# The expert results of a mixture-of-experts layer: summed in a DRAM array by the scatter, or reloaded and summed on VectorE

## The reference

```python
x = x + xattn(layernorm(x), ctx_1024, ...)      # cross attention to 4 x 4096 keys
x = x + attn(layernorm(x), ...)                 # windowed attention, 16 heads
x = x + ffn(layernorm(x), ...)                  # mixture of experts

# ffn, x_flat = [1024, 256], E = 8 experts, inner width 1024, K = 2 chosen for each token
top_v, top_i = jax.lax.top_k(x_flat @ gate_w.T, K)
probs = jax.nn.softmax(top_v)
combine = einsum('tk,tke->et', probs, one_hot(top_i, E))
for e in range(E):
    hidden = silu(x_flat @ wg[e].T) * (x_flat @ wu[e].T)
    acc += combine[e][:, None] * (hidden @ wd[e].T)
```

## Time and profile before

| what | value |
|---|---|
| time, median of 3 runs | 676.44 us (675.77 to 679.74) |
| the profiled execution: its own time | 675.65 us |
| its span, first to last instruction | 673.9 us |
| TensorE busy | 607.7 us, 90% |
| VectorE busy | 467.7 us, 69% |
| ScalarE busy | 336.0 us, 50% |
| GpSimd busy | 238.8 us, 35% |
| mean granted TensorE clock | 0.966 of full speed |
| moved by DMA | 153.61 MB, 228 GB/s over the span |

### The profile page before, as it was taken

The page is one execution under the profiler, slowest core; times in us unless marked ns, Lnnn a source line. Parts: engine busy times, 40 slices in busy tenths (PEclk is TensorE's granted clock), DMA queues, the critical chain, the costliest instruction groups (busy, mean ns, idle before and its releaser), DMA issues. The chain is left out here.

```text
span 673.9 us, 10790 instructions
## 1 busy us (share of the span) xinstructions
PE 607.7 (90%) x3988; PEld 515.9 (77%) x3988; DVE 467.7 (69%) x815; ACT 336.0 (50%) x597; POOL 238.8 (35%) x315
## 2 busy tenths in 40 slices
PE   7997999899989999998988864899999999999990
PEld 5676998699878988995656653688888888888880
DVE  4387659757876688767876857577677677677644
ACT  3434742463247524554666660465565565565530
POOL 3002862377218732784643423022222221221210
PEclk9999999999999999998999976899999999999996
DMA  8977689768977937571000334689899999999726
GB/s 280 290 273 219 191 257 354 204 175 245 341 209 201 262 95 218 147 198 39 1 1 2 126 125 157 239 312 343 320 356 342 326 352 341 326 353 337 289 79 195
DMA packets 64996, 153.61 MB, mean 228 GB/s; under 512 B 7728, under 2 KB 45168, under 8 KB 54064
## 3 DMA queue, kind: packets, MB, share of 16 engines
q1 hardware_dynamic: 62736, 146.89, 65.5%
q0 software_dynamic: 2208, 6.03, 2.4%
HBM read 122.56 MB, written 30.34 MB: 227 GB/s over the span
## 5 line engine op out<-in xcount | busy, mean ns | idle before, releaser
L615 ACT ACTIVATE wide_high<-region_a 128x1024 fp32r<-128x1024 f32 (+1 forms) x108 | 102.3, 987 | 106.7 <-PE psum L1543 106.7
L1079 DVE TENSOR_TENSOR wide_low<-region_a,wide_high 128x1024 fp32r<-128x1024 f32 x92 | 108.4, 1221 | 21.2 <-ACT wide_high L615 21.2
L544 POOL TENSOR_TENSOR wide_low<-region_a,wide_high 128x512 fp32r<-128x512 f32 x64 | 82.7, 1294 | 17.7 <-ACT wide_high L615 13.7
L1342 PE MATMUL psum<-turned_high,wide_low 128*128 128x256 f32 x256 | 79.6, 311 | 7.6 <-POOL wide_low L544 3.8
L1557 PE MATMUL psum<-region_a,region_w 128*128 128x256 f32 x368 | 83.3, 379 | 0.3 <-ACT region_w L615 0.3
L1543 PE MATMUL psum<-wide_high,turned_low 128*128 128x512 f32 x184 | 78.8, 428 | 3.6 <-DVE wide_low L1079 2.6
L1185 PE MATMUL psum<-ident,region_s 128*128 128x128 f32 x500 | 70.7, 275 | 8.0 <-ACT region_s L662 5.5
L1557 PEld LDWEIGHTS psum<-region_a,region_w 128*128 128x128 f32 x368 | 68.2, 190 | 8.9 <-issue 0.5
L1543 PE MATMUL psum<-wide_high,turned_high 128*128 128x512 f32 x184 | 73.7, 401 | 0.0
L1543 PE MATMUL psum<-wide_low,turned_high 128*128 128x512 f32 x184 | 73.6, 400 | 0.0
L615 ACT ACTIVATE wide_high<-psum 128x512 fp32r<-128x512 f32 x64 | 34.3, 598 | 78.3 <-PE psum L1304 68.6
(11 more groups left out here) (199 smaller groups left out, 1221.0 us busy)
## 6 DMA issues: line engine op xcount, KB each, us to landing
region_a<-turned_up SPq DMA_DIRECT2D x23, 2048.0 KB, 8.5
region_a<-turned_down SPq DMA_DIRECT2D x23, 1024.0 KB
region_a<-ctx_dram SPq DMA_DIRECT2D x16, 1024.0 KB, 10.2
turned_up<-region_w SPq DMA_DIRECT2D x64, 256.0 KB, 4.1
region_w<-L_ffn_wg_dram SPq DMA_DIRECT2D x16, 512.0 KB, 6.0
region_w<-L_ffn_wu_dram SPq DMA_DIRECT2D x16, 512.0 KB, 6.0
region_w<-L_ffn_wd_dram SPq DMA_DIRECT2D x16, 512.0 KB, 5.9
turned_down<-region_w SPq DMA_DIRECT2D x32, 256.0 KB, 4.2
```

The lines of the kernel that those rows point to most:

```text
L544: nc.gpsimd.tensor_tensor(val_lo[:, g % 4], ctx_sb[n][:, g * PAIR:(g + 1) * PAIR, :], val_hi[:, g % 4].bitcast(F32), ALU.subtract).then_in ...
L615: return nc.scalar.activation(dst, src, ACT.Copy)
L1079: nc.vector.tensor_tensor(w_lo[:, g % 3], whole, w_hi[:, g % 3].bitcast(F32), ALU.subtract).then_inc(low_ready, 1)
L1342: last = nc.tensor.matmul(bank[6 + c][:, 0:NTOK], v[:, g % 4, k, c * P:(c + 1) * P], p[:, g % 2, k, :], start=g == 0 and k == 0 and m == 0 ...
```

## The change

`results_by_token` is gone. In its place stands `sums_by_token` (`sum_dram`, 1024 rows and 128 spare ones). SyncE fills its first 1024 rows from `xr` with one transfer of 1 MB, issued between `load_up(1)` and `load_up(2)`, behind a wait for `heads_added`. The scatter goes by `tokens` instead of `targets` and carries `compute_op=ALU.add`: the transfer itself adds each row to what the DRAM row holds. The first scatter waits for the fill (`sums_begun`). Two tiles that hold results of the same token never run at once, since each scatter waits for the one before, as it did. When the last has landed, one transfer copies the first 1024 rows to the output, DRAM to DRAM. The 8 loads, the 16 additions and the 8 stores are gone, and so is `targets`: the constants of the place computation now give the token at once, in two VectorE instructions. `normed_rows` has 128 spare rows instead of 64.

```diff
-SPARE = P // 2
+SPARE = P
-RESULTS = TOK * TOPK
...
-        y_dram = nc.dram_tensor("results_by_token", [RESULTS + P, D], F32).ap()
+        sum_dram = nc.dram_tensor("sums_by_token", [TOK + SPARE, D], F32).ap()
...
             load_up(1)
+            sp.wait_ge(heads_added, len(LAST_ROWS))
+            sp.dma_start(sum_dram[0:TOK, :].rearrange("(t p) d -> p t d", p=P), xr).then_inc(sums_begun, 16)
             for j in range(2, SLOT_TILES):
...
-            for t in range(TILES):
-                sp.dma_start(y_of[:, t].rearrange("p k d -> p (k d)"),
-                             y_dram[t * P * TOPK:(t + 1) * P * TOPK, :].rearrange("(p k) d -> p (k d)", k=TOPK)).then_inc(y_loaded[t], 16)
-            for t in range(TILES):
-                sp.wait_ge(out_ready, t + 1)
-                sp.dma_start(out.rearrange("b (t p) d -> p (b t) d", p=P)[:, t, :], x3n[:, t, :]).then_inc(out_stored, 16)
-            sp.wait_ge(out_stored, 16 * TILES)
+            sp.dma_start(out.rearrange("b (q r) d -> (b q) (r d)", q=P // BATCH),
+                         sum_dram[0:TOK, :].rearrange("(q r) d -> q (r d)", q=P)).then_inc(out_stored, 16)
+            sp.wait_ge(out_stored, 16)
...
                 pool.wait_ge(y_ready, j + 1)
+                if j == 0:
+                    pool.wait_ge(sums_begun, 16)
...
                 pool.indirect_dma_start(
-                    out=y_dram, out_offset=bass.IndirectOffsetOnAxis(ap=target[:, j:j + 1], axis=0),
-                    in_=yt[n], in_offset=None).then_inc(y_stored[n], 16)
+                    out=sum_dram, out_offset=bass.IndirectOffsetOnAxis(ap=token[:, j:j + 1], axis=0),
+                    in_=yt[n], in_offset=None, compute_op=ALU.add).then_inc(y_stored[n], 16)
...
-            then(nc.vector.tensor_tensor(target[:, :], beside[:, :], found[:, 1], ALU.add))
-            nc.vector.tensor_scalar(token[:, :], target[:, :], 1, None, ALU.logical_shift_right).then_inc(tokens_ready, 1)
+            nc.vector.tensor_tensor(token[:, :], beside[:, :], found[:, 1], ALU.add).then_inc(tokens_ready, 1)
...
-            for t in range(TILES):
-                dve.wait_ge(y_loaded[t], 16)
-                then(nc.vector.tensor_tensor(x3n[:, t, :], y_of[:, t, 0, :], y_of[:, t, 1, :], ALU.add))
-                nc.vector.tensor_tensor(x3n[:, t, :], x3n[:, t, :], xr[:, t, :], ALU.add).then_inc(out_ready, 1)
```

More of the change, by code:

```diff
@@ L134, in perceiver @@
         hidT, yt, silu = [hidT0, hidT1], [yt0, yt1], [silu0, silu1]
-        y_f = region_a[:, 0:2 * TILES * D]
-        y_of = y_f.rearrange("p (t k d) -> p t k d", k=TOPK, t=TILES)
         xr_t = sb("residual", TILES * D)
@@ L214, in perceiver @@
         weight = sb("weights", SLOT_TILES)
-        target, token = sb("targets", SLOT_TILES, I32), sb("tokens", SLOT_TILES, I32)
+        token = sb("tokens", SLOT_TILES, I32)
         steps = sb("steps", E)
@@ L275, in perceiver @@
         y_stored = [sem(f"y_stored{n}") for n in range(2)]
-        y_loaded = [sem(f"y_loaded{n}") for n in range(TILES)]
+        sums_begun = sem("sums_begun")
         paused = sem("paused")
-        out_ready, out_stored = sem("out_ready"), sem("out_stored")
+        out_stored = sem("out_stored")
         rooms = [pv_done, scores_done, probs_turned, *w_stored, probsT_ready, scores_out, x1_ready]
@@ L435, in _ @@
             nc.gpsimd.memset(zeros, 0.0).then_inc(consts, 1)
-            nc.gpsimd.iota(spare_row[:, :], pattern=[[0, 1]], base=RESULTS, channel_multiplier=1,
+            nc.gpsimd.iota(spare_row[:, :], pattern=[[0, 1]], base=TOK, channel_multiplier=1,
                            allow_small_or_imprecise_dtypes=True).then_inc(consts, 1)
@@ L439, in _ @@
                            allow_small_or_imprecise_dtypes=True).then_inc(consts, 1)
-            nc.gpsimd.iota(way_base[:, :].rearrange("p (n t) -> p n t", n=TOPK), pattern=[[1, TOPK], [0, TILES]], base=0,
-                           channel_multiplier=TOPK, allow_small_or_imprecise_dtypes=True).then_inc(consts, 1)
-            nc.gpsimd.iota(ways[:, :, 1].rearrange("p (n t) -> p n t", n=TOPK), pattern=[[0, TOPK], [P * TOPK, TILES]], base=-RESULTS,
+            nc.gpsimd.iota(way_base[:, :].rearrange("p (n t) -> p n t", n=TOPK), pattern=[[0, TOPK], [0, TILES]], base=0,
+                           channel_multiplier=1, allow_small_or_imprecise_dtypes=True).then_inc(consts, 1)
+            nc.gpsimd.iota(ways[:, :, 1].rearrange("p (n t) -> p n t", n=TOPK), pattern=[[0, TOPK], [P, TILES]], base=-TOK,
                            channel_multiplier=0, allow_small_or_imprecise_dtypes=True).then_inc(consts, 1)
```

## The result

The changed kernel takes 673.76 us (median of 13 runs, 670.39 to 679.19), the kernel before, run beside it, 679.47 us (13 runs, 674.26 to 682.97). The ratio is **0.9949, with a 95% interval from 0.9925 to 0.9974**: 0.5% faster, some 3.5 us (1.8 to 5.1), where the prediction said 0.8% and 5.3 us. The forecast's ratio, 0.9921, lies just outside the interval. The ratio on record is not the quotient of the two medians, which is 0.9916 (5.7 us); 13 runs of each don't fix the size to better than a microsecond or two. I had given most of the chance to "within 1%", which it is, and had taken 1% for what a measurement can tell from no change; the interval reaches only 0.25% to each side and leaves out a ratio of 1.

What follows compares the result with a forecast made beforehand. TensorE sets the loop's pace, DMA close behind; the replaced end is wholly exposed. 12.5 + 0.2 - 6.2 - 1.2 = 5.3 us less, median 676.44 to 671.1 us, range 668.3 to 677.0.

Steps and rivals of the forecast that it cites:

- within 1%: Whole kernel: the time changes by under 1% (6.8 us) either way; chance 0.68.
- The end: After the last scatter: 12.5 us of loads, additions and stores go, one DRAM copy of 6.2 us (4.8 to 8) comes.
- x: Last scatter: extra time for reading and adding its DRAM rows, 1.2 us, bounds 0.2 to 3.7, counted only once.
- The loop: Expert rounds: each adding scatter takes 0.34 us more DMA engine time, covered by idle time and slack; cost 0.
- the 0.95 that I gave as the most: Loop: sign that the DMA share rises from 0.91 to no more than 0.95.
- The slow rival: Loop: adding scatters fill the DMA engines, adding 26 to 53 us (692 to 719), from 0.9 us extra engine time; chance 0.12.
- the rate-based end of my bound: Loop: idle DMA time in a 10.0 us round, 2.3 us by rate, against 0.9 us by share.
- Cost 0, with up to 0.5 us for the range: Loop's begin: the 1.05 MB fill behind the second up load delays nothing; 0 us, at most 0.5.
- if the first gather lands late behind the fill: Loop's begin: a sign that would show the prediction wrong; the first gather was expected to be issued at about 411.5.
- The third up load: Loop's begin: sign that this load is issued at about 423.9, where it was 424.12.
- Rival 1: End: x at 0.25 and the copy at 4.8 us, gain 7.6 us, 668.8 us; chance 0.20.
- Rival 3: End: the copy costs what it replaces, 676.4 us; chance 0.06.

Runs made afterwards that it cites:

- the plain scatter: The changed kernel with a scatter that overwrites instead of adding; ratio to the kernel before 0.9933.
- one more adding scatter: The changed kernel with a second adding scatter, of zeros into its own array, in each of the first 21 rounds; ratio to the kernel before 0.9959.
- the early fill: The changed kernel with the fill of the sums issued ahead of the wait for the owners, not behind the second up load; ratio to the kernel before 0.9938.
- the three kernels with more dummy products and the new scatter: The changed kernel with six TensorE dummy products instead of four, 0.9964; with fill ahead of the owners' wait and five, 0.9919, repeated 0.9929.
- The fill alone: The kernel before plus the 1 MB fill at the changed kernel's place, into an array nobody reads; first scatter waits for it; ratio 1.0048.
- the four adding scatters with the gather ahead: The changed kernel with three extra adding scatters in each of the first 21 rounds, each round's gather issued before them; ratio to the kernel before 1.0245.
- the old scatter (with five dummies): The kernel before with five TensorE dummy products instead of four ahead of the first turn; ratio 1.0011.
- Early fill and five dummy products: The changed kernel with the fill ahead of the owners' wait and five TensorE dummy products instead of four; ratios to the kernel before 0.9919, repeated 0.9929.

## Why the prediction was off

**The end: right, with the copy a little cheaper.** The 12.5 us taken away are 12.5 (12.9 with the closing 0.4). The copy was put at 6.2 us, from 4.8 to 8; it took 5.5, of which 2.0 are fixed by the line above, an estimate.

**The adding scatter: right.** x was put at 1.2 us and is 1.3, half of it in GpSimd's instruction, and it counts once. That the read would overlap the work on other rows, for which x was put near its lower bound, was my estimate; no run shows the overlap by itself. That only the last one would count also held: with the plain scatter the rounds take 214.89 us, with the adding one 214.74.

**The loop: the time right, the sizes wrong.** Cost 0 held. But I sized an adding scatter as a doubled plain one, 0.68 us of engine time, and it is more: 14.5% of 185 us is 26.8 us; less 18 gathers of 0.34 this leaves 1.1 us for each of 19 scatters. The packets go with it. The queue's packets on the page went from 2208 to 4416, and are 2208 again with the plain scatter: 48 for each gather or plain scatter on the mean, 144 for an adding one, as many as its 128 rows and the 16 engines together. So the share rose to 0.98, over the 0.95 that I gave as the most, and the up loads' worst case left 0.8 us (12.6 from issue to first use, 11.8 to landing).

**The slow rival: rightly set aside, but by the wrong threshold.** By the share, an estimate, a row costs an engine 1.1 us / 9 packets = 0.12 us, not 0.5; no row here shows directly how two additions overlap. I said that the rival decides from 0.9 us of extra engine time at the earliest. The change itself added 0.75, and one more adding scatter came to 1.9 with 0.8 us lost in all 21 rounds. With four, 4.0 us over the plain one, the program lost 20 us even with the gathers ahead, but there GpSimd's time had run out too. So 0.9 us was too low; no run shows where the threshold lies above 1.9, and the rate-based end of my bound, 2.3 us, isn't contradicted. The rival's times were also added up wrongly: 26 to 53 us on top of the forecast's 671.1 are 697 to 724, and my 692 to 719 took the gain of 5.3 us off twice.

**The step that failed** is "Cost 0, with up to 0.5 us for the range", for the fill where the loop begins, and its ground, that the gather "shares the engines with `load_up(1)` either way, and the fill is behind that". The fill cost 0.9 us of the stretch in the changed kernel (1.1 with the 0.2 us that the removed instruction gave back) and 0.8 us in the kernel before. I had shown that no load was late behind it and took a place in SyncE's queue for a place in time. The fill's own length was forecast well: it was to end 12.2 us behind the place computation and landed 12.3 us behind it (issued at 415.61, 12.3 us to landing, counted from 415.57). That its traffic and the first gather's would meet had no price. The prediction had named this sign, "if the first gather lands late behind the fill", and it came; so did a DMA share over 0.95. The third up load was to come 0.2 us earlier; counted from the place computation it came 1.8 us later (15.8 us behind it instead of 14.0).

**What stays open.** Put together, the profiles give 12.5 + 0.2 - 5.5 - 1.3 - 1.2 = 4.7, and 4.9 with the small differences in the rounds, against a forecast of 5.3. So the copy gave 0.7 us more than forecast, and the late gather's 1.2 took that and more. The runs give 3.5, from 1.8 to 5.1. The 1.4 us between them are within that interval, but they have a pattern: in the early fill, the plain scatter and the kernel with one more adding scatter, too, the ratio shows 0.8 to 1.5 us less gain than the profile counted from `spare_or_way`, and in the three kernels with more dummy products and the new scatter 2.6 to 2.8 us less. The fill alone and the four adding scatters with the gather ahead go the same way, by 3.0 and 4.0 us. These signs are not independent, since the ratios of one batch share the same runs of the kernel before, and they hang on how the runs are summed up: by the medians the changed kernel gains 0.8 us more than its profile shows, and the early fill, the plain scatter, the one more adding scatter and the three with more dummy products 0.1 to 1.6 us less. The second profile of the old scatter (with five dummies) has 263.94 us from there to the end, like the first with 263.75, so it is not one odd profile of before. The rest would have to lie ahead of that instruction, where the profiles spread over 9 us with the clock and one of each kernel can't show 1 us, or in executions unlike the profiled ones. It stays open.

Rival 1 (a better end) did not come: copy and x together are 6.8 us, over the 5.9 from which the gain passes 1%. Rival 3, with its chance of 0.06, was a copy that costs what it replaces, with a time of 676.4 us. No row or run shows a rate or a fixed cost that would make a copy so long; it took 5.5 us where 12.5 went away.

**The better version.** Early fill and five dummy products make it 0.9919 and 0.9929 to the kernel before. In both measurements the upper end is below 1; against the changed kernel the difference is likely but not settled.

## What to carry to other kernels

A tail of loads, sums and stores can become one DRAM copy behind adding scatters: here 12.5 us became 5.5, for 1.3 us more on the last scatter. Ask what the adding scatters cost in the steady loop twice over, in DMA engine time (here a packet a row) and in GpSimd's own time (1.6 us for each instead of 1.0), and which small transfer shares their queue. Put the array's first fill where the DMA engines are idle: behind a load in another queue it still delays an urgent gather, here by 0.8 to 1.4 us. Then read the granted clock of the stage that gets its data earlier; here the earlier gather by itself brought nothing to the first scatter (34.33 us after 34.37, with a clock of 0.59 after 0.79).

## What was not expected of the hardware

- A transfer issued behind a 2 MB load on SyncE's queue delayed a gather on GpSimd's queue that was issued 1.3 us after it, by 0.8 to 1.4 us (queue 0 moved 22 packets in the time in which it had moved 137). The load had landed only at 424.4, when the gather's wait was over, and the fill landed at 427.9.
- The first tile's granted clock over 8 us was 0.59, 0.66, 0.79 or 1.00. With five dummy products and the gather at 6.3 us it was busy up to 0.4 us before the turn and got 1.00 twice; with 0.6 us of idle time and the old scatter it got 0.79. With four dummy products the gather that came 1.1 us earlier went with 0.59, and the first tile took back what it gave. Why it falls one way or the other is open.
- A copy of 1.05 MB between DRAM arrays took 5.5 us and one of 0.13 MB 2.4 us, by a line through both, an estimate, 2.0 us and 296 GB/s. Pieces of 1 KB were as fast as 64 KB (5.4 us).
